# Three-product down projections for the last 24 pairs, two banks for the last up projections, and a first scan with some of its work on TensorE

## The chip, the cores and the metric

One core of one Trainium2 chip runs the whole program. The metric is the device time of one execution in microseconds (us). Where it says PE, DVE, ACT, POOL and SP, the engines TensorE, VectorE, ScalarE, GpSimd and SyncE are meant; PEld is TensorE's weight load.

## What is computed

`x` has 4096 tokens (4 sequences of 1024) of 512 features, in float32. Two residual blocks follow each other:

```
mod = silu(c) @ wmod                       # six rows of 512 per sequence; ga, gb clamped away from zero
h   = layernorm(x) * (1 + ca) + sa
u   = causal 4-tap depthwise convolution of h (+ bias)
dt, B, C = u @ xproj_w.T                   # 128 + 16 + 16 columns
delta = softplus(dt @ dtproj_w.T + b)
state[d, n] = exp(delta * A[d, n]) * state[d, n] + delta * B[n] * u[d]     # along the tokens, 16 states n
y   = sum_n C[n] * state[:, n] + u * D_skip
x   = x + ga * y
h   = layernorm(x) * (1 + cb) + sb
scores = softmax over the 2 largest of tanh(h @ Wg1.T) @ Wg2.T             # 8 experts
out = sum_e scores[e] * (silu(h @ Wup[e].T + bup[e]) @ Wdown[e].T + bdown[e])   # 256 hidden columns an expert
x   = x + gb * out
```

## The kernel before

**Tiling.** The tokens are cut into 8 chunks (`NC`) of 512 (`CT`). A chunk's recurrence is 64 slots: 16 states times 4 tiles of 128 features, in each slot one DVE scan over 512 columns (L1047). ACT makes the decay exp(delta*A) into PSUM one slot ahead (`da`, L856, banks 0 and 1), POOL makes delta*B*u up to two slots ahead (`dbu`, L677, a ring of 4), and PE transposes the states six slots later (`flip`, L1220) so that DVE can add C times the state onto the token rows of `ACC` (`acc`, L1070). The skip term `u * D_skip` is four more flips of `U` and four more `acc`. The last chunk (`SPLIT`) has its slots cut so that the first 256 tokens are finished half way (L1052).

**The feed-forward part** goes in half chunks of 256 tokens (`cs`, 0 to 15) and in pairs (`p`, 0 to 7, one for each expert), each pair two blocks of 128 hidden columns (`m`). A block is: `up`, 12 products in float32r (high and low parts of the operands, L1269 to L1271) of 256 columns into one half of bank 5; `th`, a tanh on ACT (L937); `ys` on DVE, (up + bias) times the expert's score row `SR` (L1112); `t1` on ACT (L942); `g` on POOL (L698), which gives silu times score; and `dn`, for each of two token tiles one float32 product of 512 columns of `G` and `WD`, which the trace shows as two passes (L1288). `DN` are banks 6 and 7 and hold the sum over all 16 blocks. After the last pair `to` (DVE, L1123) multiplies with gb, `fin` (POOL, L703) adds it onto `ACC` and `out` stores it. The router (`fst` to `sw`) prepares the scores of a half chunk.

**The order is written out by hand.** `schedule()` gives each task a place on one axis, two places to a slot, 128 to a chunk; each engine runs its tasks in the order of the places, and waits on semaphores only hold it back. All queues are in order, SP's too: its DMA issues (`sr`, `wd`, `br`, `out`, `xa`) wait one behind the other. The tables `ATTENTION`, `TAPS`, `ROUTER`, `PAIR`, `FAST`, `PAIRS`, `FAST_PAIRS` and `TAIL_PAIRS` hold the places. Half chunks 12 and 13 are placed beside the last chunk's scans (`FAST`), half chunks 14 and 15 after them (`TAIL_PAIRS`).

**Buffers that the change touches.** `up` of a pair waits until `ys` of the pair before has read bank 5 (L1264). `g` uses a ring of 3, `wd` a ring of 3 pairs. `hm`, `u3`, `conv`, `cvs` and `cva` are the normalized input, its first tap on ACT, and the other taps either on DVE (`conv`, L1014) or on ACT and POOL (`cvs`, L790, and `cva`, L631). `work_bank` deals out PSUM banks 2 to 6 in the head and 2 to 4 afterwards. `gbclamp` clamps gb as four rows of 512 on DVE (L948 to L954). In the first chunk POOL and ACT also split the up weights into high and low parts (`wlo`, L662, and `whi`, L878), and four small products a slot (`warm`, L1158) keep PE going.

Of the kernel before, what the change touches and what calls it, by code (L numbers as in the profile page):

```python
# [6 lines left out]
CT, FT = 512, 256  # L7
# [32 lines left out]

HEAD_TAPS = ((0, 2), (0, 1), (1, 2), (0, 0), (2, 2), (1, 1), (3, 2), (2, 1), (1, 0), (3, 1), (2, 0), (3, 0))

# [15 lines left out]
    "split": {"fst": (-43, -41), "nmf": -40, "fsu": (-39, -39), "frs": -37, "fxn": (-35, -33), "ftr": (-33, -31),
             "fev": (-32, -27), "hh": -25, "hl": (-23, -21), "r1": -25, "r12": -23, "r2": -21, "r22": -20, "r3": -19,
             "r31": -18, "e1": -17, "r4": -18, "r40": -16, "r41": -15, "r42": -12, "sel1": -13, "sel2": -12,  # L60
             "r5": -7, "r52": -8, "sw": -6}}
# [5 lines left out]
        "to": (18, 18), "fin": (21, 26), "out": (15, 29), "gbl": 22, "xa": 29}  # L67
# [18 lines left out]
WARM = {"begin": 32, "proj": 4, "slot": 4}  # L86

# [48 lines left out]

def ffn_places(cs, p):

    c, odd = divmod(cs, 2)
    pair = FAST if c == NC - 2 else PAIR  # L140
# [4 lines left out]
    for i, h in enumerate(pair["dn"]):  # L145
# [11 lines left out]
def head():  # L157
# [4 lines left out]
    a += [(what, 0, dt) for dt in range(4) for what in ("hm", "u3")]  # L162
# [12 lines left out]
def schedule():  # L175
# [41 lines left out]
    for c in range(NC):  # L217
        for j, h in SKIP if c else SKIP0:
# [24 lines left out]
def adaln_kernel(nc, x, pvec, alog, ct, wmod, xpT, dtT, wg1T, wg2T, wupT, bup, wdT, bdn, out):  # L243
# [4 lines left out]
    with ctx:  # L248
# [1081 lines left out]
```

## Time and profile before

| | |
|---|---|
| median of 3 runs | 1459.13 us (1456.96 to 1460.66) |
| profiled execution, its own time | 1456.78 us |
| its span, first to last instruction | 1455.0 us |
| PE busy | 1342.0 us, 92% |
| DVE busy | 1209.1 us, 83% |
| POOL busy | 1134.5 us, 78% |
| ACT busy | 939.6 us, 65% |
| mean granted TensorE clock | 0.968 |

The busy shares are averages over stages that have different limits, so the stages have to be looked at one by one. The first slot of a scan starts at 45.9 us, the second chunk's scans start near 183 us, the last chunk's near 1126 us, and the last scan ends at 1303 us; what follows until 1455 us is the end of the feed-forward part. Overlapped matmuls make a busy time longer than the time from one start to the next; where the cost of a product matters, the distance between starts counts.

### The profile page before, as it was taken

To read this page: it belongs to the slowest core of one execution; us is meant where nothing else is said; L and a number is where in the kernel's file an instruction comes from. 1 tells how busy PE (TensorE), PEld (TensorE's weight loads), DVE (VectorE), ACT (ScalarE), POOL (GpSimd) and SP (SyncE) were. 2 spreads that over 40 slices of the span, in tenths; PEclk is the share of its full clock that TensorE was granted. 3 is DMA by queue.
4 is the path that set the end of the run, shared out by engine and by line. 5 is a ranking of instruction groups with operands and counts; after the bars stand their busy time and mean duration, and the time that the engine had idled before them with its cause. 6 is when DMAs were issued, how large, how long until landed. Compare 5 with 4: busy or idle time off the path is not lost. (4 is left out here: it accounts for less than half of the span.)

```text
span 1455.0 us, 22897 instructions
## 1 busy us (share of the span) xinstructions
PE 1342.0 (92%) x7368; PEld 938.4 (64%) x7368; DVE 1209.1 (83%) x1717; ACT 939.6 (65%) x1949; POOL 1134.5 (78%) x1159
## 2 busy tenths in 40 slices
PE   8586767999999999999999999999999999998998
PEld 3264545667766775667667776677667766666665
DVE  4899999899998999899988999899989997882211
ACT  3684786578847785579748885679657764633211
POOL 1699889789997989798988999798979887652222
PEclk9799967999999999999999999999999999999999
DMA  5441122234342423334343434353333423233242
GB/s 203 158 146 53 34 66 88 92 96 145 101 128 98 156 89 118 123 109 132 89 142 105 154 90 135 88 156 103 111 114 96 131 77 120 94 112 102 70 127 69
DMA packets 99247, 160.88 MB, mean 111 GB/s; under 512 B 9244, under 2 KB 33948, under 8 KB 99128
## 3 DMA queue, kind: packets, MB, share of 16 engines
q1 hardware_dynamic: 99128, 159.42, 35.4%
q8 instruction: 59, 0.97, 0.3%
q14 instruction: 60, 0.49, 0.1%
HBM read 150.60 MB, written 8.79 MB: 110 GB/s over the span
## 5 line engine op out<-in xcount | busy, mean ns | idle before, releaser
L677 POOL TENSOR_TENSOR DB<-DU,BR 128x512 f32<-128x512 f32 x448 | 578.8, 1306 | 49.0 <-DVE H L1047 25.0
L1288 PE MATMUL pb<-WD,G 128*128 128x512 f32 x1024 | 482.4, 594 | 0.0
L1070 DVE SCALAR_TENSOR_TENSOR ACC<-pb,CTM,ACC 128x512 f32<-128x512 f32 x512 | 374.4, 732 | 56.9 <-PE pb L1220 56.2
L856 ACT ACTIVATE pb<-DELP,AN 128x512 f32<-128x512 f32 x448 | 307.1, 686 | 147.5 <-DVE H L1047 145.4
L1220 PE MATMUL pb<-ID,H 128*128 128x128 f32 x2048 | 320.4, 283 | 38.7 <-DVE ACC L1070 36.3
L1220 PEld LDWEIGHTS pb<-ID,H 128*128 128x128 f32 x2048 | 246.7, 145 | 165.0 <-issue 91.3
L698 POOL TENSOR_TENSOR G<-TY 128x256 f32<-128x256 f32 x256 | 189.7, 744 | 203.0 <-DVE TY L1112 125.3
L1269 PE MATMUL pb<-H2H,WUH 128*128 128x256 f32 x1024 | 321.9, 314 | 22.0 <-DVE TY L1112 22.0
L1047 DVE TENSOR_TENSOR_SCAN H<-pb,DB 128x512 f32<-128x512 f32 x256 | 309.5, 1210 | 12.2 <-ACT pb L856 11.7
L1271 PE MATMUL pb<-H2H,WUL 128*128 128x256 f32 x1024 | 291.1, 284 | 0.0
L1270 PE MATMUL pb<-H2L,WUH 128*128 128x256 f32 x1024 | 290.7, 284 | 0.0
L1288 PEld LDWEIGHTS pb<-WD,G 128*128 128x128 f32 x1024 | 179.7, 191 | 141.3 <-issue 139.8
L1047 DVE TENSOR_TENSOR_SCAN H<-pb,ST,DB 128x512 f32<-128x512 f32 x192 | 244.1, 1271 | 6.5 <-ACT pb L856 6.3
L937 ACT ACTIVATE TY<-pb,BUPH 128x256 f32<-128x256 f32 x256 | 106.9, 468 | 217.5 <-PE pb L1271 214.3
L1269 PEld LDWEIGHTS pb<-H2H,WUH 128*128 128x128 f32 x1024 | 196.7, 192 | 51.3 <-issue 27.7
L1112 DVE SCALAR_TENSOR_TENSOR TY<-pb,BUP,SR 128x256 f32<-128x256 f32 x256 | 110.8, 474 | 125.2 <-ACT TY L937 97.7
L1270 PEld LDWEIGHTS pb<-H2L,WUH 128*128 128x128 f32 x1024 | 197.3, 193 | 7.4 <-issue 7.2
L1271 PEld LDWEIGHTS pb<-H2H,WUL 128*128 128x128 f32 x1024 | 196.7, 192 | 0.0
L942 ACT ACTIVATE TY<-TY 128x256 f32<-128x256 f32 x256 | 103.5, 413 | 0.0
L1052 DVE TENSOR_TENSOR_SCAN H<-pb,ST,DB 128x256 f32<-128x256 f32 x128 | 88.3, 730 | 0.1
L680 POOL TENSOR_TENSOR DB<-DU,BR 128x512 f32<-128x512 f32 x64 | 81.4, 1284 | 1.2 <-DVE H L1052 1.1
L1014 DVE SCALAR_TENSOR_TENSOR U<-DELP,PV,U 128x512 f32<-128x512 f32 x61 | 62.8, 1040 | 2.0 <-ACT U L780 1.8
(168 smaller groups left out, 1441.1 us busy)
## 6 DMA issues: line engine op xcount, KB each, us to landing
WD<-in_wdT SPq DMA_DIRECT2D x128, 512.0 KB, 5.1
BR<-bscr SPq DMA_DIRECT2D x112, 256.0 KB, 3.9
SR<-sscr SPq DMA_DIRECT2D x128, 128.0 KB, 4.6
DU<-in_x SPq DMA_DIRECT2D x8, 1024.0 KB, 6.7
ACC<-in_x SPq DMA_DIRECT2D x16, 512.0 KB, 3.8
out<-ACC SPq DMA_DIRECT2D x32, 256.0 KB, 2.1
BR<-bscr SPq DMA_DIRECT2D x32, 128.0 KB, 3.2
DU<-in_xpT SPq DMA_DIRECT2D x8, 320.0 KB, 3.1
```

The lines of the kernel that those rows point to most:

```text
L677: eng.tensor_tensor(DB[:, i % NDB], DU[:, c % 2, r], BR[:, n % 2], ALU.mult).then_inc(S["dbu"], 1)
L698: eng.tensor_tensor(G[:, i % NG], TH[:, m % 2], YS[:, m % 2], ALU.mult).then_inc(S["g"], 1)
L856: eng.activation(DA[i % NDA][:], DEL[:, c % 2, r], ACT.Exp, scale=AN[:, r, n:n + 1]).then_inc(S["da"], 1)
L937: eng.activation(TH[:, m % 2], up_of(m), ACT.Tanh, scale=0.5, bias=BUPH[:, m:m + 1]).then_inc(S["th"], 1)
L1047: eng.tensor_tensor_scan(H[:, (c * NS + n) % NH, r], DA[i % NDA][:], DB[:, i % NDB], ST[:, n, r:r + 1] if state_from(c, h) else 0.0, ALU.mult,
L1070: eng.scalar_tensor_tensor(out=acc, in0=banks[bank_of["flip", c, n, r]][:], scalar=1.0 if n < 0 else CTM[:, c % 2, j, st:st + 1], in1=acc, ...
L1112: eng.scalar_tensor_tensor(out=YS[:, m % 2], in0=up_of(m), scalar=BUP[:, m:m + 1], in1=SR[:, m // 2 % 2], op0=ALU.add, op1=ALU.mult).then_ ...
L1220: t = eng.transpose(b[:, dt * 128:dt * 128 + 128], src[:, dt, r * 128:r * 128 + 128], ID[:])
L1269: eng.matmul(b, WUH[:, kk, sl], H2H[:, cs % 2, kk], start=kk == 0, stop=False)
L1270: eng.matmul(b, WUH[:, kk, sl], H2L[:, cs % 2, kk], start=False, stop=False)
L1271: t = eng.matmul(b, WUL[:, kk, sl], H2H[:, cs % 2, kk], start=False, stop=kk == 3)
L1288: eng.matmul(DN[j][:], G[:, (cs * NM + m) % NG, j * 128:j * 128 + 128], WD[:, (cs * NE + m // 2) % NWD, m % 2], start=False, stop=m == NM ...
```

## The change

1. From half chunk 13 on (24 pairs) `dn` is three float32r products in place of one float32 product. `wh` (ACT) and `wl` (DVE) make the high and low parts of a pair's down weights, `gh` (ACT) and `gl` (DVE) those of `G`. Their tiles lie over `DU`, `U` and `DELP`. `dn` goes to 14 and 16 places behind the pair's start; `wd` and `g` wait for `wl` and `gl` instead of `dn`.
2. From pair 4 of half chunk 14 on, every other pair's `up` writes bank 0 (`DA[0]`), which is free once the scans are over, and waits for the pair two before.
3. In the first chunk the skip term is made by PE: `skx` brings `ACC` into PSUM through the identity, `skp` adds the four tiles of `U`, and ACT copies it back (`skc`). `acc` of state 0 waits for that. Two of the four feature tiles of the second chunk's convolution are made by PE too, with diagonal matrices (`diag` on ACT, `cpe`, `cpq`), and `U` is then taken from PSUM by ACT. gb is clamped as 128x16 after a transpose and turned back (`gbt`, `gbm`, `gbb`, `gbe`). Until the second chunk's first scan, all five banks 2 to 6 are dealt out.
4. New places: for the second chunk (`ATTENTION1`, `TAPS1`), the routers of half chunks 13 to 15, `FAST`, `FAST_PAIRS`, `TAIL_PAIRS`, a table `TAIL` for half chunks 14 and 15, and `out` in `PAIR`.

```diff
-PAIR = {..., "fin": (21, 26), "out": (15, 29), "gbl": 22, "xa": 29}
-FAST = {"sr": 1, "wd": 3, "up": (0, 2), "th": (3, 3), "ys": (4, 4), "t1": (3, 4), "g": (5, 7), "dn": (9, 13),
-        "to": (15, 17), "fin": (15, 18), "out": (20, 26), "gbl": 17, "xa": 19}
+PAIR = {..., "fin": (21, 26), "out": (20, 28), "gbl": 22, "xa": 29}
+FAST = {"sr": -4, "wd": -5, "up": (0, 2), "th": (3, 3), "ys": (4, 4), "t1": (5, 5), "g": (4, 7), "dn": (10, 13),
+        "to": (14, 19), "fin": (20, 26), "out": (31, 34), "gbl": 21, "xa": 11}
+TAIL = {"sr": -1, "wd": 1, "up": (-3, -2), "th": (4, 4), "ys": (7, 7), "t1": (4, 7), "g": (7, 7), "dn": (16, 16),
+        "to": (18, 18), "fin": (16, 25), "out": (20, 34), "gbl": 17, "xa": 34}
-FAST_PAIRS = [50, 58, 64, 70, 74, 79, 84, 89, 99, 104, 110, 114, 124, 131, 137, 141]
-TAIL_PAIRS = [53, 64, 73, 78, 89, 96, 106, 117, 126, 136, 141, 151, 160, 167, 175, 184]
+FAST_PAIRS = [51, 58, 64, 72, 77, 82, 86, 96, 101, 108, 112, 117, 122, 127, 133, 138]
+TAIL_PAIRS = [69, 74, 86, 91, 118, 126, 130, 135, 143, 149, 157, 166, 169, 179, 186, 196]
+SPLIT_FROM = (13, 0)
+LOW = {"wh": (5, 5), "wl": 11, "gh": (7, 8), "gl": (11, 12), "dn": (14, 16)}
+SPARE_FROM = (14, 4)
+CONV_PE1 = ((2, (45, 47, 50, 51), 53), (3, (51, 55, 57, 59), 61))
+SKIP_PE = {0: ((0, 3, 6, 11), (1, 4, 8, 14), (2, 4, 9, 11), (3, 9, 12, 14))}
+TAPS1 = [(43, 0, 2, None), (47, 0, 1, 44), (49, 0, 0, 47), (51, 1, 2, None), (54, 1, 1, None), (59, 1, 0, 58)]
...
+        def up_of(cs, m):
+            return (DA[0] if in_spare(cs * NE + m // 2) else banks[5])[:, m % 2 * FT:m % 2 * FT + FT]
+        def up_free(eng, i):
+            if in_spare(i) and not in_spare(i - 2):
+                eng.wait_ge(S["scan"], max(nth["scan", NC - 1, NS - 1, r] for r in range(4)))
+                return
+            before = i - 2 if in_spare(i) or in_spare(i - 1) else i - 1
+            if before >= 0:
+                eng.wait_ge(S["ys"], 2 * before + 2)
...
+                elif what == "diag":
+                    for dt in sorted(pe_tiles(1)):
+                        for tap in range(4):
+                            t = eng.activation(diag_of(dt)[:, tap], ID[:], ACT.Copy, scale=par(dt, tap))
+                elif what == "wh":
+                    if half == 0:
+                        if in_parts(i - 2):
+                            eng.wait_ge(S["dn1"], 2 * (i - 2) + 2)
+                        ...
+                    eng.activation(WDH[:, i % 2, half], WD[:, i % NWD, half], ACT.Copy).then_inc(S["wh"], 1)
+                elif what == "gh":
+                    eng.wait_ge(S["g"], i + 1)
+                    if in_parts((i - 4) // 2):
+                        eng.wait_ge(S["dn1"], i - 3)
+                    eng.activation(GHL[:, 0, i % 4], G[:, i % NG], ACT.Copy).then_inc(S["gh"], 1)
+                elif what == "wl":
+                    eng.tensor_tensor(WDL[:, i % 2], WD[:, i % NWD], WDH[:, i % 2].bitcast(f32), ALU.subtract)...
+                elif what == "gl":
+                    eng.tensor_tensor(GHL[:, 1, i % 4], G[:, i % NG], GHL[:, 0, i % 4].bitcast(f32), ALU.subtract)...
...
+                    if in_parts(cs * NE + m // 2):
+                        if j == 0:
+                            eng.wait_ge(S["wl"], nth["wl", cs, m // 2])
+                            eng.wait_ge(S["gl"], nth["gl", cs, m])
+                        hi, lo = [GHL[:, w, i % 4, j * 128:j * 128 + 128] for w in range(2)]
+                        eng.matmul(DN[j][:], hi, WDH[:, i // 2 % 2, m % 2], start=False, stop=False)
+                        eng.matmul(DN[j][:], hi, WDL[:, i // 2 % 2, m % 2], start=False, stop=False)
+                        eng.matmul(DN[j][:], lo, WDH[:, i // 2 % 2, m % 2], start=False, stop=m == NM - 1)...
```

## Rows read from the trace of the kernel before

**Rows 1.** Busy time by stretch: length, then PE, PEld, DVE, ACT, POOL, clock, DMA, GB/s.
```profile
46.00:183.00 137.00, 96.96 (x560) 70.33 (x560) 129.47 (x144) 90.59 (x156) 121.61 (x99) 0.86 0.30 95
260.00:1126.00 866.00, 844.84 (x4773) 596.08 (x4772) 793.24 (x1085) 626.24 (x1283) 769.12 (x781) 1.00 0.38 116
1126.00:1303.00 177.00, 165.25 (x928) 118.90 (x927) 156.93 (x278) 102.95 (x263) 130.18 (x139) 0.98 0.35 107
1303.00:1455.00 152.00, 139.31 (x694) 93.94 (x693) 30.86 (x74) 37.39 (x99) 39.66 (x52) 0.99 0.30 91
```
**Rows 2.** PE's waits, 1303 to 1455 us: us in total, times, longest.
```profile
PE pb L1269 <- DVE TY L1112: 6.9, 8, 4.2
```
**Rows 3.** Timeline of PE after the scans: start, duration, engine, line, tiles, count.
```profile
1350.64 0.28 PE L1270 MATMUL pb<-H2L,WUH 128*128 128x256 f32 x1
1350.75 0.28 PE L1271 MATMUL pb<-H2H,WUL 128*128 128x256 f32 x1
...
1353.38 3.60 PE L1288 MATMUL pb<-WD,G 128*128 128x512 f32 x8
...
1401.15 0.39 PE L1282 MATMUL pb<-BDN,STR 96*128 96x512 f32 x1
1401.39 1.02 PE L1288 MATMUL pb<-WD,G 128*128 128x512 f32 x2
```
**Rows 4.** Weight loads in the same stretch, same columns.
```profile
1347.21 0.19 PEld L1270 LDWEIGHTS pb<-H2L,WUH 128*128 128x128 f32 x1
1347.33 0.19 PEld L1271 LDWEIGHTS pb<-H2H,WUL 128*128 128x128 f32 x1
```
**Rows 5.** Single lines of the kernel: duration ns min/median/max, first and last start, forms.
```profile
L1027 DVE TENSOR_TENSOR DELP<-DELP,DU x4: 669/684/693, 41.6 to 48.4; 128x512 f32<-128x512 f32 x4
L994 DVE TENSOR_TENSOR BDN<-XT,BDN x1: 1244/1244/1244, 82.3 to 82.3; 32x512 fp32r<-32x512 f32 x1
L909 ACT ACTIVATE H2H<-XT x16: 1043/1050/1057, 215.3 to 1338.8; 128x1024 fp32r<-128x1024 f32 x16
L942 ACT ACTIVATE TY<-TY x256: 398/414/426, 242.6 to 1444.1; 128x256 f32<-128x256 f32 x128
```
**Rows 6.** Busy time by stretch around the last scans, columns as in Rows 1.
```profile
1250.00:1275.00 25.00, 24.05 (x143) 17.10 (x141) 19.91 (x32) 14.30 (x33) 15.74 (x16) 1.00 0.26 79
1275.00:1303.00 28.00, 25.20 (x124) 17.66 (x124) 26.65 (x53) 12.34 (x33) 17.37 (x18) 0.94 0.40 128
```
**Rows 7.** Timeline of ACT, DVE and POOL, one pair near the end.
```profile
1430.43 0.84 ACT L937 ACTIVATE TY<-pb,BUPH 128x256 f32<-128x256 f32 x2 [4.86 <-PE pb L1271]
1431.38 0.88 DVE L1112 SCALAR_TENSOR_TENSOR TY<-pb,BUP,SR 128x256 f32<-128x256 f32 x2 [5.43 <-ACT TY L937]
1431.94 1.41 POOL L698 TENSOR_TENSOR G<-TY 128x256 f32<-128x256 f32 x2 [4.90 <-ACT TY L942]
```
**Rows 8.** Timeline of DVE and of SP's queue where score rows come late.
```profile
1204.20 0.34 SPq L565 DMA_DIRECT2D out<-ACC  x1
1209.17 0.88 DVE L1112 SCALAR_TENSOR_TENSOR TY<-pb,BUP,SR 128x256 f32<-128x256 f32 x2 [5.75 <-DMA SR<-sscr]
1254.88 0.88 DVE L1112 SCALAR_TENSOR_TENSOR TY<-pb,BUP,SR 128x256 f32<-128x256 f32 x2 [2.80 <-DMA SR<-sscr]
1334.35 1.59 SPq L565 DMA_DIRECT2D out<-ACC  x2
1336.04 0.38 SPq L558 DMA_DIRECT2D SR<-sscr  x1
```
**Rows 9.** Timeline of DVE and POOL early in the first chunk.
```profile
56.38 1.19 DVE L948 TENSOR_SCALAR ACC<-ACC 4x512 f32<-4x512 f32 x1
60.69 1.64 DVE L954 SCALAR_TENSOR_TENSOR ACC<-ACC 4x512 f32<-4x512 f32 x1
63.54 1.27 POOL L677 TENSOR_TENSOR DB<-DU,BR 128x512 f32<-128x512 f32 x1 [1.76 <-DVE H L1047]
75.27 0.19 POOL L592 TENSOR_SCALAR NA<-NB 128x4 f32<-128x4 f32 x1 [2.00 <-ACT JUNK L746]
```
**Rows 10.** DVE by line, 62 to 183 us: busy us, mean ns, idle before.
```profile
L1014 DVE SCALAR_TENSOR_TENSOR U<-DELP,PV,U 128x512 f32<-128x512 f32 x7 | 7.1, 1015 | 0.0
L1070 DVE SCALAR_TENSOR_TENSOR ACC<-pb,ACC 128x512 f32<-128x512 f32 x4 | 2.7, 674 | 0.0
```
**Rows 11.** Busy time by stretch in the first chunk, columns as in Rows 1.
```profile
100.00:120.00 20.00, 10.35 (x51) 7.87 (x50) 19.33 (x22) 11.11 (x18) 20.00 (x16) 0.76 0.30 101
```

More of the change, by code:

```diff
@@ L109, in attention_places @@
     at = []
-    for what, places in ATTENTION.items():
+    for what, places in (ATTENTION1 if c == 1 else ATTENTION).items():
         if what == "ldx" and c < 2:
@@ L134, in router_places, with in_parts, in_spare @@
     return at
+def in_parts(i):
+    return i >= SPLIT_FROM[0] * NE + SPLIT_FROM[1]
+def in_spare(i):
+    return i % 2 == 1 and i >= SPARE_FROM[0] * NE + SPARE_FROM[1]
 def ffn_places(cs, p):
     c, odd = divmod(cs, 2)
-    pair = FAST if c == NC - 2 else PAIR
+    pair = FAST if c == NC - 2 else TAIL if c == NC - 1 else PAIR
     b = (FAST_PAIRS if c == NC - 2 else TAIL_PAIRS if c == NC - 1 else PAIRS)[NE * odd + p]
@@ L217, in schedule @@
     for c in range(NC):
+        if c in SKIP_PE:
+            for j, begun, made, taken in SKIP_PE[c]:
+                place(2 * W * c + begun, ("skx", c, j))
+                place(2 * W * c + made, ("skp", c, j))
+                place(2 * W * c + taken, ("skc", c, j))
+            continue
         for j, h in SKIP if c else SKIP0:
@@ L327, in adaln_kernel @@
         WM = [WD0, H[:, 2], XT[:].rearrange("p (k d) -> p k d", k=4), WD0, DEL[:, 1], DU[:, 1]]
+        WDH = nc.alloc_sbuf_tensor_at("WDH", [128, 2, 2, D], f32r, offset=at_du)
+        WDL = nc.alloc_sbuf_tensor_at("WDL", [128, 2, 2, D], f32r, offset=at_u)
+        GHL = nc.alloc_sbuf_tensor_at("GHL", [128, 2, 4, FT], f32r, offset=at_delp)
         GR0, GR1 = ACC[0:4, 8], ACC[0:4, 9]
         RW = [ACC[0:4, i] for i in (2, 3, 6, 7, 2)]
-        first = set(head())
+        DGX = [z.rearrange("p s (k m) -> p (s k) m", k=2) for z in (SR[:], G[:, 0:2])]
         order = schedule()
@@ L346, in adaln_kernel @@
             if what in EMPTIED:
-                b = min(range(2, 7) if task in first else range(2, 5), key=lambda b: last[b])
+                early = at[EMPTIED[what][0], *k] < at["scan", 1, 0, 0]
+                b = min(range(2, 7) if early else range(2, 5), key=lambda b: last[b])
                 bank_of[task], freed[task] = b, held[b]
@@ L371, in work_bank, with upto, skip_done, diag_of @@
             return banks[bank_of[task]]
+        def upto(what, c):
+            return sum(1 for t in nth if t[0] == what and t[1] <= c)
+        def skip_done(c):
+            if c in SKIP_PE:
+                return S["skp"], nth["skp", c, SKIP_PE[c][-1][0]]
+            return S["flip"], nth["flip", c, -1, 1]
+        def diag_of(dt):
+            return DGX[dt - 2]
         def rows_done(g):
@@ L1066, in _ @@
                         eng.wait_ge(S["d_xa1"], 16 * (c + 1))
+                    if n == 0 and c in SKIP_PE:
+                        eng.wait_ge(S["skc"], nth["skc", c, j])
                     if nth[task] > 2:
```

194 lines of the change are left out of this document (152 added, 42 removed), and 3 rows, old and new, of the table ATTENTION1.

## The prediction

> **What bounds the kernel now.** I read the busy time by stretch first, since the page's shares mix stages. From 260 to 1126 us PE is busy 845 of 866 us at full clock [rows 1]: the middle is bound by PE, and the change leaves its work as it is. In the first chunk, 46 to 183 us, PE is busy 97 of 137 us, DVE 129.5 and POOL 121.6: two engines share the bound. Beside the last scans (1126 to 1303 us) PE is at 165 and DVE at 157 of 177. After them only PE has work, 139 of 152 us, DVE, ACT and POOL below 40 each. There the view of waits gives 6.9 us of PE waiting for `ys` [rows 2]; another 6 us is the `to`, `fin`, `out` at the very end. So a product saved after the scans counts fully, one saved beside the last scans counts only while DVE keeps up, and the first chunk gains only as far as DVE and POOL both gain.
>
> **Down projections.** Eight passes of L1288, one pair, take 3.44 us (3.60 with the drain of the last, [rows 3]), 0.43 us each, so one float32 product is 0.86 us. The same timeline has `up` products in float32r of 256 columns starting 0.11 to 0.12 us apart, and one of 512 columns (L1282) followed 0.24 us later by its successor. The added products are of that last form. From below: twice the 256-column step less its fixed part, or half a float32 pass, 0.43/2 = 0.215. From above: 0.24. I take 0.22, nearer to the pass, because the 512-column stream is what both have in common. Three are 0.66 against 0.86: 0.20 saved, 0.8 us a pair, 19 us for 24 pairs; by the ends 13.4 to 20.6 us. The weight loads do not add to it: loads of 0.19 us start 0.12 us apart beside running products [rows 4].
>
> **What it costs elsewhere, per pair.** ACT: `wh` two copies of 128x512, half of L909's 1.05 us each with some fixed time, 1.1 together; `gh` two at 0.41 like L942 [rows 5]: 1.9 us. DVE: L1027 subtracts or adds 512 columns in 0.68 us when POOL is idle, so `wl` (1024 columns) is 1.2 and `gl` 2 x 0.4, 2.0 us; L994, the same kind of operation beside a running POOL, took 1.24 us, 0.56 more. Three such instructions a pair give 2.0 to 3.7 us; I take 3.0 beside the scans. The Trainium skill bears on this ("SBUF — State Buffer", section "SBUF: two separate sides"): a DVE instruction with two SBUF inputs and a GpSimd instruction exclude each other for a whole instruction. L994 against L1027 agrees with it; by the rule in full, each of the three would wait for up to a whole POOL product, and the scans' end would come some 4 us later than I say below.
>
> **Beside the last scans.** Only pairs placed so that `wl` and `gl` fall before place 128 count: those at 101, 108 and 112, three pairs, 9 us of DVE. From 1250 to 1303 us DVE was busy 46.6 of 53 [rows 6], 6.4 free: the last scan comes 2.6 us later. PE does not mind as such: in that stretch it loses one pair's `dn` (3.44) and gains one `up` block (1.4), and saves 3 x 0.8. From both ends: DVE at 2.0 a pair, no delay; at 3.7 with ACT held by `wh`, which waits for a `dn` placed up to two places later while `da` of the next slot stands behind it, 8 us. Earlier in this chunk the new `FAST` takes `sr` four places ahead and `out` behind the next pairs. Now `sr` stood behind an `out` that waits for `fin`, and DVE waited 5.75 and 2.80 us for score rows [rows 8]. PE idles 11.8 us in the whole stretch [rows 1]; of DVE's 8.6 I count 3 us as gained, bounds 0 and 8. `wd` now stands in front of `sr` and can hold SP for `dn`; `br` has two states of lead.
>
> **After the scans.** Before: 152.0 us, 139.3 busy. Work: +2.0 (moved in, from above) - 21 x 0.8 = 124.5. Waits of PE: the five of about 0.25, one of 0.34 and one of 1.13, in total 2.7 of the 6.9 [rows 2], go with the second bank and with `sr` of half chunk 15 placed ahead of `out`. The one of 4.2 us stays: the first `sr` of half chunk 14 is still behind `out` of half chunk 13 (41 and 44 against 68), which is behind `fin` [rows 8], and pair 1's `up` still uses the only bank. New: `dn` needs `g`, `gh`, `gl`. From the end of `up` a pair takes ACT 0.84, DVE 0.88 and POOL 1.41, overlapped, to about 3.2 us [rows 7]; with `wh` ahead of the second `t1`, `gh` and `gl` it becomes about 4.2 to the first `dn` and 5.5 to the second. PE has in between, by the places, the `dn` of one or two earlier pairs at 2.64 and an `up` of 2.86: covered, except for about 0.3 at the last pair and 0.5 where `ftr` waits for the router. That makes 12.7 - 2.7 + 0.8 = 10.8 idle, and the stage 135.3: 16.7 us less. The end (`to`, `fin`, `out`) is unchanged.
>
> **The first chunk.** DVE loses four clamps on 4x512, 5.9 us from 56.4 to 62.3 [rows 9], for five on 128x16 at about 0.16 (-5.0); the four skip sums, 2.7; and four of seven taps at 1.015, 4.1 [rows 10]: 11.8 us. POOL loses only two `cva` of 1.27, and it was full from 100 to 120 us [rows 11]. What it can give back before is its idle time, 1.76 and 2.00 us and two smaller waits [rows 9], 4.7 in total: at most 7.2 us. Against it stand eight `diag` copies on ACT, about 0.2 each, in the first slot, where DVE already waited for `da`. I take 5 us, bounds 0 and 8. PE gets 16 passes of 0.43 and, for the skip, 4 x (0.86 + 0.9): 14 us at full clock, 28 at half, beside 40 idle us. `skc` and the PSUM reads replace work of like size on ACT. `out` five places later in `PAIR` I put at nothing: PE's waits in the middle do not come from there; -2 to +2.
>
> **Sum.** -5 (first chunk) - 3 (score rows) + 2.6 (later last scan) - 16.7 (after the scans) = -22.1. From the profiled execution's own 1456.8 this gives 1434.7; the median of the runs is 2.3 above it, so 1437.
>
> **Rivals.**
> 1. *The products are as saved, but the preparation holds the pairs (slower).* Point of decision: `dn` of a pair can't start until `th`, `wh`, `t1`, `g`, `gh`, `wl`, `gl` are through, 4.2 + 1.3 us, and if waits chain (`gh` and `wh` wait for the `dn` two pairs before, `g` for `gl` three blocks before) nothing overlaps: a pair costs 2.64 + 5.5, about 8.1 in place of 6.3 now and 5.5 forecast. Over the 16 last pairs +29 against now, with the other terms -5 -3 +3: 1483. If only the half of the pairs chain, 1463. For it: four slots of `GHL` and two of `WDH` only. Against it: `dn` is two pairs behind `up` by the places, and ACT and DVE are below 25% busy there. 5%.
> 2. *Weight loads add to the products (slower).* 3 x (0.19 + 0.215) = 1.2 us against 0.86, +1.4 us a pair, +33: with the rest about 1486. Rows 4 speak against it. 1%. The Trainium skill ("TensorE: Matmul & The Clock Gate", Part 3, "The mechanism") says that weight loads overlap running products only for other row groups; by it this rival would hold; this trace contradicts it, for loads and products of the whole array do overlap.
> 3. *Only the tail pays.* DVE and ACT beside the last scans cost 8 us and the first chunk gives nothing, since POOL and `diag` take it back: 1456.8 + 0 - 1 + 8 - 16.7 = 1447, as a median 1449. For it: POOL at 20.00 of 20.00 in its stretch. 17%.
> 4. *More than that.* Score rows come on time and take all of their waits with them (-7), the 4.2 us go too, the first chunk gives 8: 1456.8 - 7 - 8 + 1 - 20 = 1423, as a median 1425. 15%.
> 5. *Nothing moves*, because the old idle of PE takes the savings. After the scans there is none to speak of. 3%.
>
> The forecast has the remaining 59%. The range 1426 to 1448 takes in most of rivals 3 and 4 and leaves 2 in 10 out. A measurement of this kernel tells about 0.3% (4.4 us) from no change: faster by more than that 0.91, within it 0.04, slower 0.05.
>
> **What would show it.** L1288's float32 passes go from 1024 to 832, and a float32r product of 512 columns starts every 0.22 us. From the last scan to the end about 135 us, PE waits there about 5 us, with one of 4 us after half chunk 14's first `up`. The second chunk's first scan comes at about 178 in place of 183 us. 260 to 1126 keeps its length of 866 us, shifted. DVE waits for SR near the start of half chunk 13 are gone. Wrong would be: PE waiting for `gl` or `wl` pair after pair; products 0.3 us apart or more; last scan more than 8 us later relative to the chunk's start than the 177 us of now.

## The result and the profile after

| | before | after |
|---|---|---|
| median, us | 1458.86 (4 runs, 1456.96 to 1460.66) | 1442.02 (4 runs, 1439.28 to 1443.53) |
| profiled execution, own time | 1456.78 | 1442.15 |
| its span | 1455.0 | 1440.4 |
| PE busy | 1342.0 | 1337.2 |
| mean granted TensorE clock | 0.968 | 0.971 |

The ratio of the times is 0.9883, interval 0.9863 to 0.9902: 17 us faster. The forecast was 22 us faster, 1437; the time lies inside its range. Between the two profiled executions the difference is 14.6 us, and it is these that can be taken apart.

The page of the changed kernel, busy time by engine and the line of the products that stayed float32:

```profile
PE 1337.2 (93%) x7512; PEld 964.4 (67%) x7512; DVE 1258.5 (87%) x1782; ACT 985.7 (68%) x2056; POOL 1140.5 (79%) x1157
...
L1498 PE MATMUL pb<-WD,G 128*128 128x512 f32 x832 | 393.6, 593 | 0.0
```

The passes went from 1024 to 832, as the change says. DVE has 49 us more work than before (1209.1) and ACT 46 us more (939.6). Now the same stretches as [rows 1], columns as there; the middle and the two after it are shifted by the 7 us that the first chunk gained:

```profile
46.00:176.00 130.00, 104.45 (x608) 76.89 (x606) 120.94 (x137) 94.47 (x168) 116.14 (x96) 0.89 0.33 106
253.00:1119.00 866.00, 844.91 (x4775) 596.28 (x4774) 792.95 (x1085) 626.20 (x1283) 769.45 (x781) 1.00 0.38 116
1119.00:1297.00 178.00, 163.13 (x952) 121.72 (x950) 164.12 (x287) 111.22 (x283) 130.66 (x139) 0.98 0.35 106
1297.00:1440.40 143.40, 128.30 (x764) 111.73 (x764) 81.97 (x137) 71.94 (x175) 50.30 (x52) 0.96 0.32 97
```

The first chunk is 7 us shorter, the middle 866 us as before with PE at 844.9, the stretch beside the last scans 1 us longer, and what follows them 143.4 us in place of 152.0: -7 + 0 + 1 - 8.6 = -14.6. In the last stretch PE's work fell from 139.3 to 128.3 us, but its idle time rose from 12.7 to 15.1, and its clock fell from 0.99 to 0.96.

PE's waits in that stretch, after (us in total, times, longest), to be held against [rows 2]:

```profile
PE pb L1468 <- DVE TY L1274: 6.9, 2, 5.0
PE pb L1489 <- DVE GHL L1266: 3.1, 5, 1.1
PE pb L1428 <- ACT XT L1015: 0.7, 2, 0.4
```

The total for `ys` is the same 6.9 us as before, now in two waits instead of eight, and 3.1 us for `gl` are new. The chain of waits shows what the two for `ys` hang on (start, duration, what ran):

```profile
1297.01 0.86 DVE TY L1274 x2
1297.91 0.38 PE pb L1468
...
1327.05 0.70 DVE XT L1285
1327.82 2.54 POOL ACC L813 x2
1330.81 5.67 DMA SR<-sscr
1336.51 0.89 DVE TY L1274 x2
1337.44 0.58 PE pb L1468
```

And PE's timeline, with the idle time before an instruction and what ended it in brackets:

```profile
1297.91 0.38 PE L1468 MATMUL pb<-H2H,WUH 128*128 128x256 f32 x1 [1.90 <-DVE TY L1274]
...
1321.80 0.47 PE L1489 MATMUL pb<-WDH,GHL 128*128 128x512 f32 x1 [1.13 <-DVE GHL L1266]
...
1337.44 0.58 PE L1468 MATMUL pb<-H2H,WUH 128*128 128x256 f32 x1 [5.00 <-DVE TY L1274]
```

Read the chain from below: PE's `up` waits for `ys`, which waits for a score row whose transfer took 5.67 us, and this could not be issued before the `out` of half chunk 13, which waits for the `fin` on POOL. That is the wait of 4.2 us that the forecast expected to stay, at 5.0 us. And it does not end with the wait. The stretches right around it, columns as in [rows 1]:

```profile
1337.40:1340.00 2.60, 2.56 (x12) 2.57 (x13) 0.92 (x1) 1.76 (x4) 0.91 (x2) 0.50 0.59 161
1340.00:1343.00 3.00, 3.00 (x15) 2.73 (x15) 1.60 (x3) 0.42 (x1) 0.89 (x1) 0.50 0.47 171
```

From 1337.4 to 1343.0 PE works without a pause at a granted clock of 0.50, the 1.2 GHz level: 5.6 us for what takes 2.8 at 2.4 GHz. It stays there until 1343.5. And there is a second such stretch, which begins a microsecond after the first `ys` wait has ended at 1297.91; the kernel before has only one after its scans, from 1342.5 to 1346.0, behind its wait of 4.2 us. First the changed kernel, then the one before:

```profile
1299.50:1302.50 3.00, 3.00 (x11) 2.54 (x10) 2.32 (x5) 0.00 (x0) 0.73 (x1) 0.50 0.41 134
```

```profile
1343.00:1345.50 2.50, 2.50 (x8) 1.45 (x6) 0.00 (x0) 0.00 (x0) 0.82 (x1) 0.50 0.72 216
```

With their edges PE works at half clock for 3.4 + 6.2 us in the changed kernel and for 3.4 us before, so the clock costs 4.8 us of working time against 1.7.

The new products, from PE's timeline, one full run of them:

```profile
1383.48 0.39 PE L1489 MATMUL pb<-WDH,GHL 128*128 128x512 f32 x1
1383.71 0.39 PE L1490 MATMUL pb<-WDL,GHL 128*128 128x512 f32 x1
1383.94 0.40 PE L1491 MATMUL pb<-WDH,GHL 128*128 128x512 f32 x1
...
1387.65 0.28 PE L1468 MATMUL pb<-H2H,WUH 128*128 128x256 f32 x1
```

Eighteen products fill 1383.48 to 1387.65: 4.17/18 = 0.232 us from start to start. Three are 0.695 us against 0.86 for a float32 product.

What prepares them, single lines of the changed kernel (duration min/median/max in ns, first and last start, forms):

```profile
L1260 DVE TENSOR_TENSOR WDL<-WD,WDH x24: 1199/1226/2121, 1268.9 to 1429.8; 128x1024 fp32r<-128x1024 f32 x24
L1266 DVE TENSOR_TENSOR GHL<-G,GHL x48: 396/426/1230, 1270.0 to 1432.0; 128x256 fp32r<-128x256 f32 x48
L1064 ACT ACTIVATE WDH<-WD x48: 611/625/636, 1259.5 to 1429.1; 128x512 fp32r<-128x512 f32 x48
L1071 ACT ACTIVATE GHL<-G x48: 399/410/420, 1261.6 to 1431.6; 128x256 fp32r<-128x256 f32 x48
```

DVE's waits beside the last scans, first of after (1119 to 1297 us), then of before (1126 to 1303 us); this view of before did not stand ahead:

```profile
DVE TY L1274 <- ACT TY L1081: 8.8, 4, 3.1
DVE TY L1274 <- DMA SR<-sscr: 0.6, 1, 0.6
```

```profile
DVE TY L1112 <- DMA SR<-sscr: 9.9, 4, 5.8
DVE TY L1112 <- ACT TY L937: 7.9, 6, 2.1
```

The waits for score rows are gone (9.9 to 0.6 us), as the forecast had it. All the same the last scan starts no earlier, counted from the router's store of half chunk 11 on SP: 203.33 us after it, before 202.38.

### The profile page after: what moved, and what is told of

Read it like the earlier page. It is cut to its first block and busy times, and to the rows that moved or that the text cites. A ratio compares the mean times of both kernels' runs of the same rounds, so it can differ in the third digit from the quotient of the medians.

```text
span 1440.4 us, 23450 instructions
## 1 busy us (share of the span) xinstructions
PE 1337.2 (93%) x7512; PEld 964.4 (67%) x7512; DVE 1258.5 (87%) x1782; ACT 985.7 (68%) x2056; POOL 1140.5 (79%) x1157
## 5 line engine op out<-in xcount | busy, mean ns | idle before, releaser
L1498 PE MATMUL pb<-WD,G 128*128 128x512 f32 x832 | 393.6, 593 | 0.0
L808 POOL TENSOR_TENSOR G<-TY 128x256 f32<-128x256 f32 x256 | 199.5, 780 | 182.1 <-DVE TY L1274 136.3
L1468 PE MATMUL pb<-H2H,WUH 128*128 128x256 f32 x1024 | 316.6, 309 | 23.0 <-DVE TY L1274 23.0
L1193 DVE TENSOR_TENSOR_SCAN H<-pb,DB 128x512 f32<-128x512 f32 x256 | 309.5, 1210 | 15.1 <-ACT pb L983 13.0
L1498 PEld LDWEIGHTS pb<-WD,G 128*128 128x128 f32 x832 | 144.8, 190 | 109.3 <-issue 108.3
L1320 PE MATMUL pb<-H2H 128*128 128x256 f32 x292 | 59.0, 335 | 3.0 <-ACT H2H L835 3.0
```

Source lines behind the costliest of these rows:

```text
L808: eng.tensor_tensor(G[:, i % NG], TH[:, m % 2], YS[:, m % 2], ALU.mult).then_inc(S["g"], 1)
L1193: eng.tensor_tensor_scan(H[:, (c * NS + n) % NH, r], DA[i % NDA][:], DB[:, i % NDB], ST[:, n, r:r + 1] if state_from(c, h) else 0.0, ALU.mult,
L1468: eng.matmul(b, WUH[:, kk, sl], H2H[:, cs % 2, kk], start=kk == 0, stop=False)
L1498: eng.matmul(DN[j][:], G[:, (cs * NM + m) % NG, j * 128:j * 128 + 128], WD[:, (cs * NE + m // 2) % NWD, m % 2], start=False, stop=m == NM ...
```

## The experiments

All kernels but the version before are the changed kernel with the edits shown. Since every run shifts as a whole with its first chunk, each profiled execution is cut at two marks: the issue of the `sscr` store of half chunk 11 and the start of the last scan; the end is the issue of the last `out`. The store of half chunk 0 tells how long the first chunk took.

| kernel | store of half chunk 0 | store of 11 to last scan | last scan to last `out` | ratio to before |
|---|---|---|---|---|
| before | 229.99 | 202.38 | 149.40 | 1 |
| changed | 223.28 | 203.33 | 140.83 | 0.9883 |
| one float32 product again | 221.68 | 206.92 | 151.61 | 0.9971 |
| one bank for `up` | 221.26 | 203.19 | 163.92 | 1.0062 |
| both, and the old places at the end | 221.57 | 205.66 | 153.71 | 0.9989 |
| no low parts | 223.90 | 198.84 | 130.88 | 0.9807 |
| three products from half chunk 14 | 222.34 | 205.88 | 143.18 | 0.9933 |
| first score rows of half chunk 14 early | 222.13 | 203.26 | 135.02 | 0.9841 |
| the same, second bank from its start | 222.47 | 203.42 | 133.20 | 0.9839 |
| the same, three products from (13, 3) | 224.38 | 203.26 | 131.69 | 0.9823 |
| old queue order in `FAST` | 224.11 | 206.37 | 138.25 | 0.9898 |
| skip sums back on DVE | 223.63 | 203.38 | 138.35 | 0.9887 |
| convolution back on DVE | 226.38 | 203.17 | 136.79 | 0.9911 |

The stages come from one profiled execution each, and what lies between the stores of half chunks 0 and 11, the same work in all, is in no column: 866.6 to 870.8 us, and 874.5 in the kernel with one float32 product, whose profiled execution was the slowest of its ten. The first column differs by some 2 us between kernels with the same first chunk (221.3 to 224.4), so a difference of that size in one column says little by itself; the ratios come from alternated runs.

The second column is steadier: six kernels with the same places there have 203.2 to 203.4. The third is not. The changed kernel and the last three of the table have the same end, and yet 140.8, 138.3, 138.4 and 136.8 us. The wait before the second pair's `up` is 5.00, 4.02, 4.16 and 4.05 us in them, and PE's clock is at 0.50 after the last scan (the idle end left out) for some 10, 7, 7 and 3.5 us. These two account for the differences to within 0.6 us. So a difference of up to 4 us in the third column can come without any edit at that end.

**One float32 product instead of three.**

```diff
-SPLIT_FROM = (13, 0)
+SPLIT_FROM = (16, 0)
-    for i, h in enumerate((LOW if parts else pair)["dn"]):
+    for i, h in enumerate((LOW if parts or cs >= 13 else pair)["dn"]):
```

> The changed kernel with every down projection as one float32 product again, at the places of the three (14 and 16 behind the pair's start); no high and low parts are made. Theory A (the three products save what the distances between starts say, 0.86 - 3 x 0.232 = 0.165 us a token tile and block, 15.8 us for 24 pairs; making the parts costs about 3 us of waits after the scans and 2 beside them): 10 to 12 us slower than the changed kernel's 1442, about 1453. Rival B (making the parts eats most of what the products save, and the gain of the change is the first chunk's): 0 to 4 us slower, 1442 to 1446.

Measured: 1453.72 us (1448.53 to 1460.35, 10 runs), ratio 0.9971 [0.9957, 0.9985]; against the changed kernel's 0.9883 that is 1.0089, 13 us slower, where 10 to 12 were expected. After the last scan it is 10.8 us longer, about what the distance of the three products says: 0.165 us x 4 x 21.5 pairs = 14.2 us, less the 3.1 us of waits for `gl`. But the last scan too comes 3.6 us later, although DVE has no low parts to make:

```profile
1301.08 0.74 POOL L808 TENSOR_TENSOR G<-TY 128x256 f32<-128x256 f32 x1 [4.33 <-PE pb L1498]
```

With float32 products `g` waits until `dn` frees its tile, `dn` stands at the late places 14 and 16, and the scan's `db` stands behind `g` on POOL. That is a price of these places and not of the product. Three quarters of the whole gain go with this edit; not all of that is the price of the products.

**One bank for `up`.**

```diff
-SPARE_FROM = (14, 4)
+SPARE_FROM = (16, 0)
```

> The changed kernel with all up projections in the one bank 5. Theory A: before the change the one bank cost 0.25 us of PE's waits at about every other pair and more where the scores were late; with ys seven places behind and dn elsewhere I expect 2 to 4 us, 1444 to 1446. Rival: dn of older pairs covers the wait now, no difference, 1442.

Measured: 1465.78 us (1463.71 to 1468.3), ratio 1.0062 [1.0045, 1.0078]: 24 us slower than the changed kernel and slower than before. Both expectations, 2 to 4 us and no difference, missed it by far. PE's waits from 1306 to 1462 us in this kernel, and the busy times of all engines in the middle of that stretch:

```profile
PE pb L1468 <- DVE TY L1274: 19.6, 8, 4.1
PE pb L1489 <- DVE GHL L1266: 2.8, 4, 1.1
```

```profile
1345.00:1430.00 85.00, 68.37 (x368) 60.43 (x367) 36.96 (x68) 33.33 (x82) 22.61 (x22) 0.86 0.27 79
```

Eight waits for `ys` make 19.6 us, and the granted clock in this stretch falls to 0.86. The new places put some `up` close behind the one before (166 and 169 in `TAIL_PAIRS`): with one bank the later one must wait until DVE has emptied it. So the bank is no small extra that removes waits of 0.25 us, as the forecast counted it: the new places with the three products stand on it. Three products at the old places with one bank were not run, so which of the two needs the bank more is open.

**Both undone, and the old places at the end.**

```diff
-TAIL_PAIRS = [69, 74, 86, 91, 118, 126, 130, 135, 143, 149, 157, 166, 169, 179, 186, 196]
+TAIL_PAIRS = [53, 64, 73, 78, 89, 96, 106, 117, 126, 136, 141, 151, 160, 167, 175, 184]
-SPLIT_FROM = (13, 0)
-SPARE_FROM = (14, 4)
+SPLIT_FROM = (16, 0)
+SPARE_FROM = (16, 0)
-        kind = "final" if cs % 2 else "split"
+        kind = "odd" if cs % 2 else "split"
-    pair = FAST if c == NC - 2 else TAIL if c == NC - 1 else PAIR
+    pair = FAST if c == NC - 2 else PAIR
-    for i, h in enumerate((LOW if parts else pair)["dn"]):
+    for i, h in enumerate((LOW if parts or cs == 13 else pair)["dn"]):
```

> One float32 product, one bank, and for half chunks 14 and 15 the old places (pairs, tasks of a pair, router of 15); first chunk, FAST and half chunk 13's dn at 14 and 16 as in the changed kernel. Theory A (the new end places and the second bank bring nothing by themselves, they only make room for the longer chain): last scan as in the run with one product and new places, and from there the 149.4 us of the kernel before against 151.6: 1 to 3 us faster than that run. Rival (places and bank are worth something of their own): 3 us or more slower than it.

Measured: 1454.49 us (1451.35 to 1459.81, 7 runs), ratio 0.9989 [0.9972, 1.0006]. The expected gain of 1 to 3 us over the first experiment is not there; the intervals overlap. For float32 products with one bank the old places are as good as the new ones with two banks. Both kernels keep `dn` of half chunk 13 at 14 and 16, and in both POOL is held by it (here 5.99 us, and the last scan 2.3 us later than in the changed kernel).

**No low parts.** `wl` and `gl` make 16 columns only and all three products use the high parts, so the kernel leaves out the low parts of `WD` and `G`; PE's work is the same, DVE's falls.

```diff
-eng.tensor_tensor(WDL[:, i % 2], WD[:, i % NWD], WDH[:, i % 2].bitcast(f32), ...)
+eng.tensor_tensor(WDL[:, i % 2, 0, 0:16], WD[:, i % NWD, 0, 0:16], WDH[:, i % 2, 0, 0:16].bitcast(f32), ...)
-eng.tensor_tensor(GHL[:, 1, i % 4], G[:, i % NG], GHL[:, 0, i % 4].bitcast(f32), ...)
+eng.tensor_tensor(GHL[:, 1, i % 4, 0:16], G[:, i % NG, 0:16], GHL[:, 0, i % 4, 0:16].bitcast(f32), ...)
-eng.matmul(DN[j][:], hi, WDL[...], ...); eng.matmul(DN[j][:], lo, WDH[...], ...)
+eng.matmul(DN[j][:], hi, WDH[...], ...); eng.matmul(DN[j][:], hi, WDH[...], ...)
```

> The changed kernel, but the low parts are made for 16 columns only (an instruction of some 0.15 us in place of 1.2 and 0.4) and all three products use the high parts; semaphores and places are the same. It leaves out DVE's work of 2.0 to 2.6 us a pair and computes the down projections without their low parts. Theory A, as predicted (DVE's extra work beside the scans holds the last scan back by some 2 to 4 us, and PE's waits for gl after them, 3.1 us, are its length): 5 to 7 us faster than 1442 (or than 0.9883 of before). Rival (the run with half chunk 13 back in float32: the extra work is hidden beside the scans): only the 3.1 us after them, 2 to 3 us faster, last scan where it was.

Measured: 1427.91 us (1423.87 to 1431.12), ratio 0.9807 [0.9784, 0.9829], 11 us faster than the changed kernel, where 5 to 7 were expected. In its profiled execution the last scan comes 4.5 us earlier and the stage after it is 10 us shorter, with PE's waits at 5.1 instead of 10.7 us. PE's waits (1292 to 1424 us) and busy times in this kernel:

```profile
PE pb L1468 <- DVE TY L1274: 3.2, 2, 2.1
PE pb L1428 <- ACT XT L1015: 1.9, 2, 1.6
```

```profile
1291.00:1424.00 133.00, 123.02 (x764) 108.25 (x764) 47.40 (x136) 71.81 (x176) 40.73 (x52) 0.99 0.33 103
```

All 3.1 us of waits for `gl` are gone and the `ys` waits are down by 3.7, and the clock is back at 0.99. Of the 10 us, 5.6 are waits and some 5 are the clock, of which up to 3 come and go without any edit, as the table shows. So DVE, busy 82 of 143 us after the scans, is not the bound there and yet costs 7 to 10 us, for the work stands in the chain that PE waits for. The changed kernel's chain of waits shows one such place:

```profile
1318.93 0.88 DVE TY L1274 x2
1319.81 1.51 DVE WDL L1260
1321.80 0.47 PE pb L1489
```

`gl` had to wait for `wl` on DVE's queue, and PE for `gl`.

**Three products from half chunk 14 only.**

```diff
-SPLIT_FROM = (13, 0)
+SPLIT_FROM = (14, 0)
-    for i, h in enumerate((LOW if parts else pair)["dn"]):
+    for i, h in enumerate((LOW if parts or cs >= 13 else pair)["dn"]):
```

> The changed kernel with half chunk 13's eight pairs back to one float32 product, at the same places; half chunks 14 and 15 keep three. Theory A (DVE bounds the last 30 us of the scans and the low parts made there, 7.8 us, hold the last scan back): the last scan comes 3 to 5 us earlier, the eight pairs cost PE 5.3 us more, together 1441 to 1444. Rival (DVE's extra work is hidden there): the last scan stays and the time is 5 us longer, 1447.

Measured: 1447.62 us (1445.68 to 1448.21), ratio 0.9933 [0.9916, 0.9949], 7 us slower than the changed kernel. That is the rival's 1447, but the rival had the last scan stay, and the theory had it 3 to 5 us earlier: it comes 2.6 us later although DVE has less to do. Timeline of this kernel at that place:

```profile
1294.85 0.74 POOL L808 TENSOR_TENSOR G<-TY 128x256 f32<-128x256 f32 x1 [6.02 <-PE pb L1498]
...
1296.87 1.39 DVE L1198 TENSOR_TENSOR_SCAN H<-pb,ST,DB 128x256 f32<-128x256 f32 x2 [3.88 <-POOL DB L788]
```

With float32, `g` must wait for `dn` to free its tile, `dn` is placed late, and POOL stood 6.02 us in front of `g` while the scan's `db` stood behind it. Two things changed at once, so this run does not price half chunk 13's three products by itself. It shows an unforeseen use of them: `gh` and `gl` free `G` early, so POOL is not held.

**First score rows of half chunk 14 early.** Everything else unchanged, `sr` and `wd` of its first two pairs go ahead of the `out` of half chunk 13.

```diff
+    if cs == NF - 2 and p < 2:
+        at = [(12 + 10 * p, ("sr", cs, p)), (13 + 10 * p, ("wd", cs, p))]
```

> The changed kernel with the score rows and down weights of half chunk 14's first two pairs asked for ahead of the stores of half chunk 13 (places 12, 13 and 22, 23 in place of 68, 70, 73, 75; the stores are at 41 and 44). Theory A (PE's wait of 5.0 us before the second pair's up, and the 5.6 us of half clock behind it that cost 2.8, come from SP's queue): PE goes through, 5 to 8 us faster than 1442, 1434 to 1437. Rival (the router of half chunk 15 or ACT's and DVE's chain for the first pairs takes the wait over): 0 to 2 us faster.

Measured: 1435.3 us (1432.11 to 1435.95), ratio 0.9841 [0.9824, 0.9857], 6 us faster than the changed kernel, 5.8 us of it after the last scan. At the same `up`, the timeline of this kernel:

```profile
1331.87 0.39 PE L1470 MATMUL pb<-H2H,WUH 128*128 128x256 f32 x1 [1.97 <-DVE TY L1276]
```

The wait fell from 5.00 to 1.97 us and the first product behind it took 0.39 instead of 0.58. Three microseconds less of wait gave 5.8 us. Part of the rest is the clock, here for 1325 to 1350 us, first in the changed kernel, then in this one:

```profile
1325.00:1350.00 25.00, 19.32 (x109) 15.89 (x107) 8.15 (x12) 11.69 (x26) 9.98 (x11) 0.86 0.44 127
```

```profile
1325.00:1350.00 25.00, 22.35 (x140) 19.41 (x140) 11.50 (x33) 14.44 (x34) 10.77 (x10) 0.93 0.24 75
```

From 0.86 to 0.93 in 25 us is 1.8 us. Not that the clock stays up: a microsecond after the shorter wait it falls as well, but for some 3.5 us instead of 7, here in the kernel with the early rows:

```profile
1333.00:1336.00 3.00, 3.00 (x16) 3.00 (x16) 1.35 (x3) 0.83 (x2) 1.71 (x2) 0.50 0.67 204
```

Another 1.7 us is the changed kernel's half-clock stretch right behind the last scan, which this execution does not have. It lies ahead of the place where the rows matter, so the edit does not explain it. Together 3.0 + 1.8 + 1.7 is 0.7 more than the 5.8, of which 0.4 is the first `ys` wait, 2.33 us here and 1.90 there.

**The same with the second bank from the start of half chunk 14**, and then **also with three products only from pair 3 of half chunk 13**:

```diff
-SPARE_FROM = (14, 4)
+SPARE_FROM = (14, 0)
```

> The kernel with the early score rows, and the second bank used from the first pair of half chunk 14 on instead of from the fifth. Theory A (what is left of PE's wait there, 1.97 us, is the one bank): 2 to 3 us faster than the kernel with the early rows alone, ratio to the kernel before 0.982 to 0.983, about 1432 where before is 1457. Rival (another chain, the router's or the low parts', takes over): the same as early rows alone, 1435.

```diff
-SPLIT_FROM = (13, 0)
+SPLIT_FROM = (13, 3)
-    for i, h in enumerate((LOW if parts else pair)["dn"]):
+    for i, h in enumerate((LOW if parts or (cs, p) == (13, 0) else pair)["dn"]):
```

> Early score rows and the second bank from the first pair of half chunk 14, as before, and the first three pairs of half chunk 13, the only ones whose low parts DVE makes beside the scans, back to one float32 product at the old places 10 and 13 behind the pair (the very first stays at 14 and 16). Theory A (DVE's 7.8 us of low parts hold the last scan back by 4.5 us, and what spoilt the run with half chunk 13 in float32 was POOL waiting for dn in front of its dbu): last scan 4 us earlier, three pairs cost PE 2 us: 2 to 3 us faster than the kernel without this step, ratio to before 0.982. Rival (PE is as short as DVE in that stretch, so the products saved there were worth what the low parts cost): no difference, 0.984. Second rival (POOL is held by dn again): 2 us slower, 0.9855.

Measured: 1433.79 us (1430.28 to 1434.57, 5 runs), ratio 0.9839 [0.9825, 0.9853], and 1430.49 us (1428.24 to 1434.5, 5 runs), ratio 0.9823 [0.9803, 0.9844]. The bank takes the last wait at that place away (in the table 1.8 us) but the two ratios with and without it are the same. The second is the fastest version that computes all of the reference, 9 us below the changed kernel; its interval overlaps that of the first, so the step between the two is likely, not shown. And the reason given for it did not hold: the last scan was to come 4 us earlier, and it comes where it was (203.26 us in the table, 203.42 without this step). POOL was held by `dn` again, as the second rival had it, at the old places too. POOL's waits from 1250 to 1297 us, and the busy times of the last stretch of scans:

```profile
POOL G L810 <- PE pb L1500: 13.0, 4, 4.6
```

```profile
1275.00:1295.00 20.00, 16.83 (x71) 11.03 (x72) 14.34 (x24) 8.66 (x22) 10.27 (x10) 0.83 0.22 61
```

DVE is busy only 14.3 of the last 20 us of the scans there. So DVE's low parts hold the last scan back only while nothing else does; with float32 products beside the scans, PE and POOL take DVE's place.

**Old queue order in `FAST`.**

```diff
-FAST = {"sr": -4, "wd": -5, ..., "out": (31, 34), ...}
+FAST = {"sr": 1, "wd": 3, ..., "out": (20, 26), ...}
```

> The changed kernel with the old order in SP's queue beside the last scans: sr and wd one and three places behind a pair's start, out at 20 and 26. Theory A (taking sr ahead of out removed 8.6 us of DVE's waits and some 3 us of time): DVE's waits for SR come back, the last scan 2 to 4 us later, ratio to before 0.990 to 0.991. Rival (the waits turned into waits for tanh of about the same length, 7.9 before and 8.8 after, so the order is worth nothing): the last scan within 1 us, 0.988.

Measured: 1442.08 us (1440.27 to 1442.88), ratio 0.9898 [0.9878, 0.9918]; the interval overlaps that of the changed kernel. In the trace DVE waits 3.1 us for score rows instead of 0.6 and the last scan comes 3.0 us later: exactly the term of the forecast. But the next stage is 2.6 us shorter:

```profile
1299.50:1440.20 140.70, 126.49 (x764) 110.39 (x764) 82.08 (x137) 71.83 (x175) 50.47 (x52) 0.97 0.32 102
```

PE has the same 764 instructions in it as in the changed kernel, so no work has left it. Its longest wait is 4.02 us instead of 5.00, and it is at half clock only once, around that wait (0.50 from 1336.5 to 1343.0). Less wait (1.0) and 3.9 us less work at half clock (1.9) are the 2.6 and a little more. No run shows that the queue order brings this about, so it is in part chance that the ratio hardly moves.

**Skip sums back on DVE** and **convolution back on DVE.**

```diff
-SKIP_PE = {0: ((0, 3, 6, 11), (1, 4, 8, 14), (2, 4, 9, 11), (3, 9, 12, 14))}
+SKIP_PE = {}
```

> The changed kernel with the first chunk's skip term again as four flips and four sums on DVE (2.7 us). Theory A (POOL has the lead of the first chunk and DVE's 2.7 us lie where POOL has slack only in the first 35 us): 1 to 2 us slower than 0.9883 of before. Rival (DVE bounds the first chunk, each microsecond of it counts): 2.7 us slower. Second rival (skx, skp and skc hold the first sums back, and the four sums are free): 0 or faster.

```diff
-            return CONV_PE1 if c == 1 else ()
+            return ()
-    ... (ATTENTION1 if c == 1 else ATTENTION).items() ... TAPS1 if c == 1 else TAPS
+    ... ATTENTION.items() ... TAPS
```

> The changed kernel with the second chunk's convolution as before: seven taps on DVE, five on ACT and POOL, the old places of chunk 1, no diag. Theory A (first chunk: POOL full from 80 to 140 us, its two adds of 1.27 and DVE's four taps are what the convolution brings, the clamp the rest): the second chunk's rows come 2.5 to 4 us later than in the changed kernel, ratio to before 0.9905 to 0.991. Rival (the 7.1 us of the first chunk are the clamp's 5 and the skip's 2.7, and the convolution was hidden): 0 to 1 us.

Measured: skip back 1440.26 us (1439.5 to 1441.59), ratio 0.9887 [0.9872, 0.9902]: the same as the changed kernel, so the skip term on PE is worth nothing that can be measured; the 1 to 2 us of the first theory are missed. Convolution back 1442.81 us (1441.65 to 1445.15), ratio 0.9911 [0.989, 0.9931]: 4 us slower by the ratio, with intervals that still touch. Its first chunk is 3.1 us longer than the changed kernel's, in the range expected; its profiled execution ends at 1439.8 us all the same, since its wait behind the `out` of half chunk 13 is 4.05 us instead of 5.00 and it has a clock of 0.98 after the scans instead of 0.96, with no half clock right behind the last scan.

## Why the prediction was right in direction and five to seven and a half us too high in gain

**The first chunk: right.** -5 was forecast with 7.2 as the most that POOL's idle time can give back; nearly all of it came, 7.0 us. By the experiments 2 to 5 of the 7 come from the convolution and nothing from the skip sums; by difference the rest belongs to the clamps on 128x16 and the new places, which were not tried alone. That POOL's idle time was the limit is argued, not shown. The 2 us above the forecast are luck for the total. One of the five clamps took far more than the 0.16 us that each was given:

```profile
53.70 0.25 DVE L1092 TENSOR_SCALAR GBC<-GBC 128x16 f32<-128x16 f32 x1
53.99 1.19 DVE L1094 TENSOR_SCALAR GBC<-GBC 128x16 f32<-128x16 f32 x1
```

**The middle: right.** 866 us in both.

**Beside the last scans: mechanism right, sizes off by a little, +1.0 for -0.4.** Score rows on time are worth 3.0 us there, as forecast (old queue order). The three pairs' low parts take 7.8 us of DVE (three `wl` of 1511 ns and six `gl` of 545 ns on average) where 9 was forecast, but they delay the last scan by 4.5 us (no low parts), not by the 2.6 that DVE's idle time was to leave of them. A reason that fits, not tried by itself: idle time that lies ahead of the low parts does not cover them. From 1275 to 1297 us DVE is busy 21.9 of 22.0:

```profile
1275.00:1297.00 22.00, 18.09 (x116) 15.36 (x115) 21.90 (x37) 12.73 (x33) 9.21 (x10) 0.99 0.21 66
```

And one `wl` directly ahead of the last two scans is one of those that took 2.12 us instead of 1.2 (DVE's timeline):

```profile
1291.05 2.12 DVE L1260 TENSOR_TENSOR WDL<-WD,WDH 128x1024 fp32r<-128x1024 f32 x1
...
1295.71 1.38 DVE L1198 TENSOR_TENSOR_SCAN H<-pb,ST,DB 128x256 f32<-128x256 f32 x2
```

The rule of the Trainium skill ("SBUF — State Buffer", section "SBUF: two separate sides") that a DVE instruction with two SBUF inputs and a GpSimd instruction exclude each other agrees: min 1.199, median 1.226, max 2.121 us, and the one of 2.12 us, from 1291.05 on, began while POOL ran `fin` from 1290.81 to 1292.09. The other two `wl` beside the scans took 1.20 and 1.21 us, and of the six `gl` one took 1.21 us and five 0.40 to 0.42: two of nine were hit, so the 4 us that the rule in full would have cost are too much.

**After the last scans: the step that failed, -8.6 for -16.7.** The forecast had 124.5 us of PE's work and 10.8 us idle, 135.3. Measured were 128.3 and 15.1, 143.4.
- *The product.* "I take 0.22" measured 0.232, near the upper end 0.24: 12 products a pair by 21.5 pairs by 0.012 = 3.1 us. It takes the forecast's 19 us for 24 pairs to 15.8.
- *The clock.* It was in no term. PE works 9.6 us at half clock now and 3.4 before: 3.1 us more are lost.
- *"The one of 4.2 us stays."* It did, at 5.0, and 1.9 us for the first `ys` at 1297.9 came with it: that `ys` stands right behind the last scan on DVE's queue. The small ones went, 2.7 us as forecast.
- *"Covered, except for about 0.3 at the last pair and 0.5."* Waits for `gl` are 3.1 us in 5, the longest 1.13; the last pair's, at 1432.00, is 0.69. The chain of preparation is as long as worked out, but DVE's queue was left out of it: `gl` stands behind `wl` and `ys`.
- *Work moved.* +2.0 was forecast. Counted in the two windows, PE has 19.8 pairs of `up` and 20.5 of `dn` left before the change (476 products and 164 passes), 19.0 and 21.5 after it (456 and 258 products). At the forecast's own prices that is 139.3 - 0.8 x 2.86 + 3.44 - 21.5 x 0.8 = 123.2 where it had 124.5, so this part was 1.3 us too high. The four products with `BDN` in this stretch, in no term either, take 1.7 us in place of 3.2.

Together 3.1 + 3.1 - 1.3 - 1.5 = 3.4 of the 3.8 us of work, and the waits 0.8 + 1.9 + 2.8 (for `gl`, 0.3 was forecast) + 0.2 (`ftr` for `XT`, 0.7 where 0.5 was) = 5.7 more than forecast, with 1.4 us less idle time at the end: 4.3, as measured. Experiments show two of these: without low parts the waits for `gl` and the clock's loss are gone (10 us shorter, of which up to 3 can be the clock's own scatter), and with the score rows early one wait and what follows it is (-5.8 us). The product's distance is read, not tried.

**The rivals.** *Preparation holds the pairs*: not with two banks, where five waits make 3.1 us; with one bank it is what happens (+24 us), by `ys` rather than by `gl`. *Weight loads add*: refuted; starts 0.232 us apart with loads of each product between them. The Trainium skill ("TensorE: Matmul & The Clock Gate", Part 3, "The mechanism"), which the forecast cited for it, also names a background weight buffer for which a load may go ahead of running products. The trace agrees with that part of the rule, since loads for the whole array do go ahead, and the forecast gave only the other. *Only the tail pays*: half right, for what the low parts cost, but the first chunk paid in full. *More than that*: its 1425 needed the wait of 4.2 us gone; with that done, 1433.8 and 1435.3. (The range 1426 to 1448 just leaves out these two rivals' own figures, 1449 and 1425.) *Nothing moves*: refuted.

## What to carry to other kernels

When faster products shorten a stage that is all TensorE, price what prepares them on the queue in which it stands, not by its engine's busy share: 82 of 143 us busy still cost 7 to 10 us. Price a wait of TensorE together with the half-clock stretch that may follow it. And look for what a small enabling edit (a second bank) carries before counting it as small; undo it alone first.

## What was not expected of the hardware

- A float32r product of 512 columns every 0.232 us at full clock, of 256 columns every 0.12, and a float32 pass of 512 columns 0.43: three float32r products cost 81% of the two float32 passes they replace.
- After a wait of 5.0 us PE ran 6.1 us at 1.2 GHz (1337.44 to 1343.5). The first product behind a wait does not tell whether the clock falls: it took 0.38 us, as at full clock, after 4.19 us before the change, and 0.39 after 1.97 us with the score rows early, and in both PE was at 0.50 a microsecond later (1343.0 to 1345.5, and 1333.0 to 1336.0).
- The same short wait can do either. After 1.90 us behind the last scan PE fell to 0.50 from 1299.5 to 1302.5 in the changed kernel, and with the convolution back on DVE, after 1.90 us at the same `up`, it stayed at 1.00 (1301 to 1305). In the kernel with one bank, waits of 3.94, 2.47 and 4.09 us were followed by first products of 0.55, 0.58 and 0.58 us.
- A 128x16 operation on DVE took 1.19 us where its neighbours of the same size take 0.17 to 0.25. It ended at 55.18, as three products of POOL from 51.43 to 55.15 did; why it was held and the one at 53.70 was not is open.
